# Moving the routing stage's fill tables from GpSimd to VectorE, with four smaller edits, in a graph and expert layer

## The reference

```
xn = layernorm(x)
x  = x + graph_attention(xn, W, a, src, dst) + linear_attention_mix(xn, 4 weights)
xf = layernorm(x)
scores = maximum(xf @ gate_W + gate_b, 1e-4);  p = softmax(scores)      # 8 experts
the two best experts of each node; weights maximum(p, 0.1), scaled to sum 1
x  = x + sum over its two experts of weight/2 * (xf @ expert_W[e] + expert_b[e])
```

## Time and profile before

| | us |
|---|---|
| median of 3 runs (1250.13 to 1252.03) | 1251.67 |
| the profiled execution | 1250.8 |
| its span, first to last instruction | 1249.0 |
| TensorE busy in the span | 1182.7 |
| first expert product starts at | 949.85 |

### The profile page before, as it was taken

One profiled execution on the slowest core, in us unless ns is written; L12 is line 12 of the kernel. 1 busy time (PEld: TensorE's weight loads), 2 busy tenths in 40 slices (PEclk: granted clock), 3 DMA queues, 4 the chain that ended last, 5 costly groups with the idle time before them and its releaser, 6 DMA issues.

```text
span 1249.0 us, 16313 instructions
## 1 busy us (share of the span) xinstructions
PE 1182.7 (95%) x5799; PEld 992.4 (79%) x5799; DVE 734.5 (59%) x1483; ACT 325.5 (26%) x438; POOL 456.7 (37%) x447
## 2 busy tenths in 40 slices
PE   6999999999999999999999999999946999999996
PEld 5788888878788889889977878888845788777874
DVE  7979522454334677777677447997475722543434
ACT  2411212232111111111012213333242521533333
POOL 3960677878685000000000006324126344334343
PEclk9999999999999999999999999999967999999998
DMA  5101442843321322212045651253256955785855
GB/s 206 35 34 34 119 120 69 272 130 86 92 52 29 88 89 89 93 60 61 23 138 182 202 155 49 105 199 111 98 195 193 365 117 86 204 263 93 242 89 131
DMA packets 91031, 156.08 MB, mean 125 GB/s; under 512 B 14786, under 2 KB 45244, under 8 KB 90836
## 3 DMA queue, kind: packets, MB, share of 16 engines
q1 hardware_dynamic: 75556, 129.76, 30.8%
q0 software_dynamic: 15408, 25.44, 11.7%
HBM read 112.95 MB, written 42.04 MB: 124 GB/s over the span
## 4 chain that ended last, share of the span: by engine, by line
PE 83%; DVE 6%; POOL 6%; DMA 2%; issue 2%; ACT 1%; DVEq 0%; ACTq 0%; POOLq 0%; SPq 0%
PE ps L1583 25%; PE ps L1584 25%; PE ps L1585 25%; POOL in L668 4%; DVE e_lo L1427 2%; PE ps L1711 2%; PE ps L1754 2%; PE ps L1823 1%; PE ps L1670 1%; DMA e_raw<-in_L_ffn_expert_W 1%; DMA q_in<-in_L_mix_w_query_right 1%; PE ps L1623 1%; ACT e_hi L949 1%; POOL pad_c L759 1%; POOL pad_r L758 1%
## 5 line engine op out<-in xcount | busy, mean ns | idle before, releaser
L683 POOL DMA_INDIRECT tab_d<-val_i,addr_i x160 | 206.0, 1287 | 109.5 <-issue 109.5
L1583 PE MATMUL ps<-e_hi,lt_hi 128*128 128x512 f32 x368 | 149.0, 405 | 7.9 <-DVE e_lo L1427 6.2
L698 POOL TENSOR_TENSOR att_part<-att 128x640 f32<-128x640 f32 x10 | 15.8, 1577 | 365.9 <-PE ps L1585 352.6
L1585 PE MATMUL ps<-e_hi,lt_lo 128*128 128x512 f32 x368 | 144.3, 392 | 0.0
L1584 PE MATMUL ps<-e_lo,lt_hi 128*128 128x512 f32 x368 | 144.1, 392 | 0.0
L1583 PE MATMUL ps<-xt_hi,q_hi 128*128 128x416 f32 (+1 forms) x384 | 142.9, 372 | 0.0
L1584 PE MATMUL ps<-xt_lo,q_hi 128*128 128x416 f32 (+1 forms) x384 | 136.1, 354 | 0.0
L1585 PE MATMUL ps<-xt_hi,q_lo 128*128 128x416 f32 (+1 forms) x384 | 135.5, 353 | 0.0
L1260 DVE TENSOR_TENSOR cnt<-ps,cnt 128x256 f32 x208 | 87.5, 421 | 40.7 <-PE ps L1711 25.5
L784 POOL DMA_INDIRECT out<-y,row_put x46 | 73.6, 1600 | 91.2 <-ACT y L991 72.6
L1583 PEld LDWEIGHTS ps<-e_hi,lt_hi 128*128 128x128 f32 x368 | 69.5, 189 | 30.9 <-DVE e_lo L1427 14.1
(11 more groups left out here) (288 smaller groups left out, 2673.6 us busy)
## 6 DMA issues: line engine op xcount, KB each, us to landing
e_raw<-in_L_ffn_expert_W SPq DMA_DIRECT2D x64, 512.0 KB, 8.4
acc<-in_x SPq DMA_DIRECT2D x18, 512.0 KB, 8.3
w_raw<-in_L_mix_w_key SPq DMA_DIRECT2D x16, 512.0 KB, 3.7
h_d<-hs SPq DMA_DIRECT2D x18, 256.0 KB, 2.0
q_in<-q_d SPq DMA_DIRECT2D x9, 512.0 KB, 5.2
xm<-in_x SPq DMA_DIRECT2D x18, 256.0 KB
h_in<-h_d SPq DMA_DIRECT2D x9, 512.0 KB, 5.8
mix_d<-xm SPq DMA_DIRECT2D x18, 256.0 KB
```

Of the source, the lines that this page charges most:

```text
L683: nc.gpsimd.indirect_dma_start(out=tab_d, out_offset=bass.IndirectOffsetOnAxis(ap=addr_i[0:EP, j:j + 1], axis=0), in_=val_i[0:EP, j:j + 1] ...
L1583: nc.tensor.matmul(o, lh, rh, start=(k == 0), stop=False)
L1585: return nc.tensor.matmul(o, ll, rh, start=False, stop=(k == last_k))
```

## The change

Five edits:
1. The two fill tables are made by VectorE in three instructions over all experts at once, behind `tok_w` and ahead of the first block's low parts. GpSimd still works out `pad_t` and signals it (`s_padt`).
2. TensorE reads six of the nine bounds ahead of the small products and three behind the fill count's product.
3. TensorE runs 28 float32 products of a constant 128x128 tile ahead of the first node tile.
4. Half 0 is weighed by ScalarE, half 1 by VectorE. Except in the last expert, VectorE does so behind the low part of the next block's half. In the last expert both weigh as early as they can. VectorE's next `yb` waits for its own half alone.
5. Four bias buffers. Biases 2 and 3 are loaded once the slot weights are there, ahead of expert 2's rows, and expert e+3's bias when expert e begins (for e from 1 to 4).

```diff
+            sp.wait_ge(s_wslot, 1)
+            for e in range(2, NBIAS):
+                load_bias(e)
             for e in range(NE - 1):
-                if e >= 1:
+                if 1 <= e and e + NBIAS - 1 < NE:
                     sp.wait_ge(s_ye, first_block[e] * 2 + 2)
-                    load_bias(e + 1)
+                    load_bias(e + NBIAS - 1)
...
-            for e in range(NE):
-                G.tensor_scalar(pad_r[:, e, :], io16[:, :], pad_at[:, e:e + 1], None, ALU.is_equal)
-                last = G.tensor_scalar(pad_c[:, e, :], io16[:, 0:NSLOT], last_b[:, e:e + 1], pad_t[:, e:e + 1], ALU.is_equal, ALU.mult)
-            last.then_inc(s_pad, 1)
...
+                def left_weighed(i):
+                    act.wait_ge(s_sc[0], i * 16 + 16)
+                    act.wait_ge(s_ye, i * 2 + 3)
+                    act.sem_inc(s_passed, 1)
+                    nc.scalar.activation(y[:, 0:HALF], yb[:, 0:HALF], ACT.Copy, scale=w_slot[:, bass.ds(i, 1)]).then_inc(s_y[0], 1)
                 with act.Fori(first_block[e], first_block[e + 1]) as i:
+                    if e == NE - 1:
+                        left_weighed(i)
                     for h in range(NH):
-                        c = slice(h * HALF, (h + 1) * HALF)
                         act.wait_ge(s_mm, i * 3 + (2 + h))
                         block_hi(i + 1, h)
-                        act.wait_ge(s_sc[h], i * 16 + 16)
-                        act.wait_ge(s_ye, i * 2 + (3 + h))
-                        act.sem_inc(s_passed, 1)
-                        nc.scalar.activation(y[:, c], yb[:, c], ACT.Copy, scale=w_slot[:, bass.ds(i, 1)]).then_inc(s_sum2, 1)
+                        if h == 0 and e < NE - 1:
+                            left_weighed(i)
...
             last.then_inc(s_wtab, 1)
+            dve.wait_ge(s_padt, 1)
+            V.tensor_tensor(last_c[:, :, :], io16[:, 0:NSLOT].unsqueeze(1).to_broadcast([P, NE, NSLOT]),
+                            last_b[:, :].unsqueeze(2).to_broadcast([P, NE, NSLOT]), ALU.is_equal)
+            link(V.tensor_tensor(pad_r[:, :, :], io16[:, :].unsqueeze(1).to_broadcast([P, NE, P]),
+                                 pad_at[:, :].unsqueeze(2).to_broadcast([P, NE, P]), ALU.is_equal))
+            V.tensor_tensor(pad_c[:, :, :], last_c[:, :, :], pad_t[:, :].unsqueeze(2).to_broadcast([P, NE, NSLOT]), ALU.mult).then_inc(s_pad, 1)
             block_lo(0, 0)
...
+                def right_weighed(i):
+                    c = slice(HALF, D)
+                    dve.wait_ge(s_sc[1], i * 16 + 16)
+                    dve.wait_ge(s_ye, i * 2 + 4)
+                    V.tensor_scalar(y[:, c], yb[:, c], w_slot[:, bass.ds(i, 1)], None, ALU.mult).then_inc(s_y[1], 1)
...
                     for h in range(NH):
                         c = slice(h * HALF, (h + 1) * HALF)
-                        dve.wait_ge(s_sum2, i * 2 + (1 + h))
+                        dve.wait_ge(s_y[h], i + 1)
                         dve.wait_ge(s_mm, i * 3 + (1 + 2 * h))
-                        V.tensor_tensor(yb[:, c], ps[:, h, :], bias[:, e % 2, c], ALU.add).then_inc(s_ye, 1)
+                        V.tensor_tensor(yb[:, c], ps[:, h, :], bias[e % NBIAS][:, c], ALU.add).then_inc(s_ye, 1)
+                        if h == 1 and e == NE - 1:
+                            right_weighed(i)
                         block_lo(i + 1, h)
+                        if h == 1 and e < NE - 1:
+                            right_weighed(i)
...
+            pe.wait_ge(s_const, 1)
+            for _ in range(28):
+                nc.tensor.matmul(ps[:, 7, 0:P], ones[:, :], ones[:, :], start=True, stop=True)
...
-            first_block = [pe.value_load(bounds[0:1, e:e + 1], min_val=0, max_val=NBLK) for e in range(NE + 1)]
+            first_block = [pe.value_load(bounds[0:1, e:e + 1], min_val=0, max_val=NBLK) for e in range(6)]
...
             nc.tensor.matmul(ps[:, 6, 0:NE], tri2[:, :], pad_n[:, :], start=True, stop=True).then_inc(s_nonp, 1)
+            for e in range(6, NE + 1):
+                first_block.append(pe.value_load(bounds[0:1, e:e + 1], min_val=0, max_val=NBLK))
```

More of the change, by code:

```diff
@@ L192, in gps_layer @@
         y = at("y", EX + 3 * D, [P, D])
-        bias = at("bias", EX + 4 * D, [P, 2, D])
+        NBIAS = 4
         assert EX + 6 * D <= RAW
@@ L246, in gps_layer @@
         yb = at("yb", YB, [P, D])
+        bias = [at(f"bias{b}", word, [P, D]) for b, word in enumerate((EX + 4 * D, EX + 5 * D, YB + D, RAW + 3 * NT * NE))]
+        assert YB + 2 * D <= G and RAW + 3 * NT * NE + D <= YB
         slot_f = gate("slot_f", [P, NSLOT])
@@ L430, in gps_layer @@
         s_wtab, s_wsum, s_wslot = sem("s_wtab"), sem("s_wsum"), sem("s_wslot")
-        s_bias = [sem(f"s_bias{i}") for i in range(2)]
+        s_bias = [sem(f"s_bias{b}") for b in range(NBIAS)]
         s_ehi, s_elo = sem("s_ehi"), sem("s_elo")
@@ L435, in gps_layer @@
         s_passed = sem("s_passed")
-        s_put, s_sum2, s_sc = sem("s_put"), sem("s_sum2"), [sem(f"s_sc{h}") for h in range(2)]
+        s_put, s_y, s_sc = sem("s_put"), [sem(f"s_y{h}") for h in range(2)], [sem(f"s_sc{h}") for h in range(2)]
         s_gpos, s_non, s_nonp, s_pre, s_padt, s_pad, s_padp, s_rows, s_step = (sem(n) for n in (
@@ L602, in load_bias @@
             def load_bias(e):
-                sp.dma_start(bias[:, e % 2, :], expert_b[e:e + 1, :].partition_broadcast(P)).then_inc(s_bias[e % 2], 16)
+                sp.dma_start(bias[e % NBIAS][:, :], expert_b[e:e + 1, :].partition_broadcast(P)).then_inc(s_bias[e % NBIAS], 16)
             def load_target(t):
@@ L755, in _ @@
             step(G.tensor_tensor(pad_ok[:, :], pad_ok[:, :], pad_n[:, :], ALU.mult))
-            step(G.tensor_tensor(pad_t[:, :], pad_ok[:, :], tokv[:, 0:1].to_broadcast([P, NE]), ALU.mult))
-            for e in range(NE):
-                G.tensor_scalar(pad_r[:, e, :], io16[:, :], pad_at[:, e:e + 1], None, ALU.is_equal)
-                last = G.tensor_scalar(pad_c[:, e, :], io16[:, 0:NSLOT], last_b[:, e:e + 1], pad_t[:, e:e + 1], ALU.is_equal, ALU.mult)
-            last.then_inc(s_pad, 1)
+            G.tensor_tensor(pad_t[:, :], pad_ok[:, :], tokv[:, 0:1].to_broadcast([P, NE]), ALU.mult).then_inc(s_padt, 1)
             blocks = pool.value_load(bounds[0:1, NE:NE + 1], min_val=NE, max_val=NBLK)
```

8 lines of the change are left out of this document (5 added, 3 removed).

## The result

The changed kernel takes 1247.88 us (median of 16 runs, 1243.05 to 1254.69) against 1252.11 (1249.62 to 1257.21) for the kernel before on the same chip: ratio 0.9956, 95% interval 0.9942 to 0.9970. Its profiled execution took 1247.71, with a span of 1245.9.

What follows compares the result with a forecast made beforehand. TensorE, busy 1182.7 of 1249 us, was taken to bound the kernel, with one long gap before the first expert product. Terms -9.0 - 0.6 - 2.5 + 0.8 - 0.4 = -11.7 took 1250.8 to 1239.1, median 1240.0; range 1238 to 1242, chance 0.6.

Steps and rivals of the forecast that it cites:

- Fill tables: Gap before the first expert product: tables take 1.9 us on VectorE, gain 9.0, bounds 8.0 and 9.3.
- The clock at the first products: First expert products: an earlier clock rise gains 0.6 us, from 0 to 1.7 with only 1.1 let through.
- Bounds in two parts: TensorE's register reads around the small products: gain 0, at most 0.1 us, the later three reads hidden.
- Constant products: Start and Gram stage: 28 products change nothing since VectorE sets the pace; 0, with a loss of at most 2 us.
- the case at the higher clock: Kernel start: the 28 products take about half of 16.0 us, ending near 9.
- Weighing: Steps between two experts' loops: 0.5 us gained at five of seven places, together 2.5 (0 to 5.6).
- Four bias buffers, and the transfers: SyncE's queue ahead of expert 2's rows: early biases delay a late row, loss 0.8 us (0 to 3.5).
- Transfers take more back: Rival for 941 to 992: bytes set the path, biases cost the full 3.5 us; 1243.8, chance 0.18.
- The tail: Kernel end: VectorE weighs the last half at once, gain 0.4 us (0 to 1.3).
- My base: Whole kernel: terms were summed against the one profiled execution, 1250.8 us, with the median 0.9 above it.

Runs made afterwards that it cites:

- e15: The changed kernel itself measured once more, nothing altered; ratio 0.9951 to the kernel before.
- e11: The kernel before with only the weighing of halves split between ScalarE and VectorE; ratio 0.9994 to the kernel before.
- e14: The kernel before, loading only the left half of each weight row's columns from expert 2 on; worth 1.00 and 0.96 us in the two stretches.
- e6: The kernel before with the 28 constant products alone; ratio 0.9984 to the kernel before.
- e3: The changed kernel with SyncE's register reads moved early and each bias loaded behind its step's rows; 53.14 us from first expert product to expert 2's second block.
- e1: The changed kernel with two bias buffers again, loaded as before; 52.24 us against 52.61 from first expert product to expert 2's second block.
- e2: The changed kernel with SyncE's nine register reads ahead of expert 1's fourth row; 48.99 us from first expert product to expert 2's second block.
- e10: The changed kernel with early SyncE register reads and four, not five, rows of experts 2, 3 and 5 split ahead; 1240.88 us.
- e7: The kernel before with the fill tables made on VectorE alone; ratio 0.9922 to the kernel before, from seven executions.
- e9: The changed kernel, loading only the left half of each weight row's columns from expert 2 on; 1234.39 us.
- e5: The changed kernel with early SyncE register reads and without the 28 constant products; ratio 0.9916 to the kernel before.
- e8: The changed kernel with early SyncE reads, no constant products and two bias buffers; 51.98 us from first expert product to expert 2's second block.
- e4: The changed kernel without the 28 constant products; TensorE waited 3.02 us at 971 in its profile.
- e12: The changed kernel with ten constant products between experts 1 and 2; 52.58 us from first expert product to expert 2's second block.

## Why the prediction was wrong

- **Fill tables.** Right: 1.97 for 1.9, and 9.57 gained for 9.0; the weight product and its successor overlap by more than I gave them. No fill table, low part or register read held the first product.
- **The clock at the first products.** In the profile it came up at once, my higher bound; in e15 1.9 us behind the first product. Both lie within my term, and what it gave can't be told apart from the stretch to `yb` 7. VectorE's low parts held the start little (0.19 at 948.25, 0.17 at 949.39). I wrote that the clock stayed down beside the small products; in e11 and e14, which have them as before has, it came up at 941.5 and 941.4 and fell again at 944.9 and 944.8, in the idle time.
- **Bounds in two parts.** Right: the second ten products wait 0.95 for `tok_r`, the reads are hidden, gain 0.
- **Constant products.** 8.29 for the 28, as in the case at the higher clock (8; they end at 9.42). The first tile comes no later, as said. For the whole kernel e6 shows no loss in time; the 3.02 of the profile goes over my bound of 2, and it is the length of the clock's fall, which I had not in the sum.
- **Weighing.** Mechanism right, size wrong: 0.83 a step and not 0.5. VectorE's loop exit doesn't show: the low part starts with the scaling's end, 1.69 behind `yb`, where I had 2.0. The last three steps together give 2.20, where I had 1.5. But only these three kept it; I had five places, and e11 shows that the first ones turn it into waits, and more.
- **Four bias buffers, and the transfers: the step that failed.** I wrote that the late row "would come earlier by only 9 instead of 10" and took 0.8 for the loss. It came 5.3 earlier, and the loss measured 4.25 up to `yb` 7. Over expert 4's start it was another 1.17, where a step's 0.83 was to be gained; neither edit 1 nor edit 4 alone has that loss (33.39 and 33.29), and apart from e3's hint at the biases its cause is open. The bias bytes were a wrong thing to weigh for the first stretch (0.4, e1). What I missed is the lead. During the 8.86 of TensorE's idle time the transfers and VectorE's splitting of rows went on: 8 us at 238 GB/s, 1.9 MB, nearly four rows. With the gap closed that lead is gone and the same rows have to come through at 400 GB/s while TensorE uses them up. The last rows of expert 1 hang on VectorE's low parts of expert 0, and those end at 949.33 against 946.16: 3.17 later, with a shift of 3.38. TensorE moved by 9.57, these rows by 0.2. Expert 2's rows, which wait for expert 1's low parts, then came earlier by part of it only: 5.7 us for the fifth one, 5.3 for the fifth of expert 3. In before the last wait was 0.94: I read it as a small wait, and it meant that the rows had no margin left. My rival *Transfers take more back* named this with 3.5 for bytes, gave 1243.8 and had 0.18; the measured median is 4 beyond it.
- **Register reads on SyncE.** Seen in no step of mine: 5.2 us in SyncE's queue that its wait for a buffer had covered; e2 and e10 take them away.
- **The tail.** 0.14 for 0.4: the last transfer to the output starts 1.8 behind the scaled half, with "issue" as its only named cause.
- **My base.** I summed on one execution with a short fall of the clock in the Gram stage. From the gate scores on, kernels before took 330.7 and 328.7 (e6), the changed one 324.3 and 326.0 (e15): on average 4.6 less, about the 4.2 of the medians. Against the profile of before alone the terms are -9.6 at the first product, +4.3, +1.2, -2.2 and -0.1, so -6.5 in place of my -11.7. Against e6, whose stretches to `yb` 7 and `yb` 25 are 2.1 shorter together (47.18 and 32.25 for 48.36 and 33.21), they would be -4.4.

Shown: that the early start alone brings the wait and the loss (e7), that the bytes of the rows bind (e9, e14), that `yb`'s place behind a late row's low part carries it to TensorE (e10). Each stage rests on one profile for a kernel, two for before's and after's code (e6, e15). Open: what sets how long the fifth row of expert 3 takes from issue to landing (11.2 to 15.2 us in the table, with five rows ahead and all bytes); what the 1.17 at expert 4 comes from; whether the 28 products bring the long fall in the Gram stage.

## What to carry to other kernels

When a gap of the bounding engine is to be closed, ask what works ahead in it. Take the next expert's data, count the bytes that must land until each of its uses, and set it against the rate at saturation; here a remaining wait of 0.9 us meant that there was no slack, and closing the gap paid only until the first late buffer. Then look at which in-order queue carries the lateness to the engine that matters: here four rows in place of five split ahead of `yb` did more, in the profiles at hand, than moving a bias load or the register reads.

## What the runs showed of the hardware

- A wait of TensorE of 2.3 to 4.2 us among the expert products mostly went with a fall of the granted clock to 1.2 GHz, for 3.4 or 6.8 us, from within the wait or up to 1.2 us behind it (after at 974, and e1, e3, e5, e7, e8, e11), but not always: 3.24 at 1101.98 in after (1.00 from 1096 to 1112), 3.02 in e4 and 2.35 in e12 had no fall, and waits of 1.5 to 1.7 in e2, e12 and e15 had one.
- The granted clock also falls in the Gram stage in all 17 profiles, for 3.4, 6.8 or 10.2 us, in 14 of them at 60 behind a wait of TensorE of 1.4, which all 17 have; and it falls near 275 or 420 in 13 of them, which goes with 1 to 7 us more for that stage. Near 420 a wait of 2.4 to 3.5 goes with it.
- Among the expert products a fall cost 1.6 us (3.4 us down) or 2.5 to 2.8 (6.8 us down) where no late row followed, and nothing that shows where one did (after, e12).
- Nine register reads of SyncE took 5.2 us (949.70 to 954.94) without an idle row that tells of them; moved away in e2, the gap is 0.2.
- The transfers reached 400 to 424 GB/s with rows of 512 KB from one queue; beside indirect puts and gathers 310 to 363 at a share of 1.04 to 1.08.
